# A grouped convolution with two attention gates: the convolution put on eight array tiles, the column sums folded, the statistics made one unit earlier

## The reference

```python
def _gn(v, G=32, eps=1e-5):                # over 16 channels and all pixels
    return (v - mean) / sqrt(var + eps)

# per group gx [16, 128, 128] of the normed x
ch = conv1x1(concat(mean(gx), max(gx)), w_cc, b_cc)       # 32 -> 16, one value a channel
channel_weight = sigmoid(norm_over_1x1(ch, gn1_w, gn1_b))
hw = conv1x1(concat(mean over columns, mean over rows), w_s1, b_s1)
pos_h = sigmoid(conv1x1(hw[rows], w_ph, b_ph))            # one value a channel and row
pos_w = sigmoid(conv1x1(hw[columns], w_pw, b_pw))         # one value a channel and column
sx = conv3x3(gx * pos_h * pos_w, w_s3, pad 1) + b_s3      # 16 -> 16 channels
spatial_weight = sigmoid(norm_per_channel(sx, gn2_w, gn2_b))
out = x + gx * channel_weight * spatial_weight
```

## Time and profile before

| | |
|---|---|
| median of 3 runs | 4297.24 us (4292.31 to 4298.69) |
| the profiled execution, its time | 4296.2 us |
| its span, first to last instruction | 4294.3 us |
| mean granted TensorE clock | 0.965 of full speed |
| HBM read, written | 268.64 MB, 268.44 MB |

### The profile page before, as it was taken

One profiled execution on the slowest core, in us unless ns is written; L12 is line 12 of the kernel. 1 busy time (PEld: TensorE's weight loads), 2 busy tenths in 40 slices (PEclk: granted clock), 3 DMA queues, 4 the chain that ended last, 5 costly groups with the idle time before them and its releaser, 6 DMA issues.

```text
span 4294.3 us, 55492 instructions
## 1 busy us (share of the span) xinstructions
PE 4041.4 (94%) x11016; PEld 1938.2 (45%) x11016; DVE 4018.4 (94%) x2719; ACT 2624.4 (61%) x4354; POOL 1775.4 (41%) x2314
## 2 busy tenths in 40 slices
PE   5999999999999999999999999999999999999997
PEld 2444444444444444444444444444444444444443
DVE  7999999999999999999999999999999999999996
ACT  3566566666665666666656666666666666665665
POOL 3443444444434434443344434344444344434443
PEclk9999999999999999999999999999999999999998
DMA  6777777777777777777777777777777777777775
GB/s 124 163 173 173 172 175 169 175 172 173 172 173 169 177 173 172 175 167 178 172 172 172 172 176 172 171 172 176 168 177 173 172 175 167 177 173 173 171 177 123
DMA packets 1147751, 730.57 MB, mean 170 GB/s; under 512 B 74144, under 2 KB 1122976, under 8 KB 1147552
## 3 DMA queue, kind: packets, MB, share of 16 engines
q1 hardware_dynamic: 1147552, 728.87, 74.7%
HBM read 268.64 MB, written 268.44 MB: 125 GB/s over the span
## 4 chain that ended last, share of the span: by engine, by line
DVE 53%; issue 18%; SPq 11%; DMA 9%; PE 6%; POOL 1%; ACT 1%; DVEq 1%; POOLq 0%; ACTq 0%
DVE sums L560 13%; DVE mx L607 12%; SPq L222 11%; DMA xt<-in_x 9%; DVE sp_buf L524 7%; DVE sums L554 7%; DVE gated L567 7%; DVE sp_buf L527 6%; PE conv_ps L637 5%; POOL rstd L275 1%; ACT sp_buf L416 1%; DVE gate_hr L594 0%; PE pos_ps L637 0%; DVE ch L603 0%; DVE sums_n L545 0%
## 5 line engine op out<-in xcount | busy, mean ns | idle before, releaser
L637 PE MATMUL conv_ps<-gated,W_conv 128*128 128x512 f32 x6144 | 2973.1, 619 | 16.5 <-DVE gated L567 16.3
L637 PEld LDWEIGHTS conv_ps<-gated,W_conv 128*128 128x128 f32 x6144 | 1143.4, 197 | 1100.0 <-issue 1071.7
L637 PE MATMUL conv_ps<-halo,W_halo 96*128 96x512 f32 x2048 | 1027.7, 604 | 2.1 <-DMA halo<-gated 1.6
L370 ACT ACTIVATE sp_buf<-conv_ps,weights 128x1024 f32<-128x1024 f32 x512 | 565.3, 1104 | 747.8 <-PE conv_ps L637 747.5
L323 POOL TENSOR_TENSOR gated<-gate_w,gate_hr 128x2048 f32<-128x2048 f32 x256 | 918.7, 3609 | 166.9 <-DVE gate_hr L594 157.6
L560 DVE TENSOR_REDUCE sums<-xt 128x128 f32<-128x2048 f32 x256 | 943.6, 3725 | 0.0
L554 DVE TENSOR_REDUCE sums<-xt 128x16 f32<-128x2048 f32 x256 | 584.2, 2282 | 171.5 <-DMA xt<-in_x 171.4
L524 DVE SCALAR_TENSOR_TENSOR sp_buf<-xt,negm,sp_buf 128x2048 f32<-128x2048 f32 x256 | 600.6, 2346 | 38.3 <-ACT sp_buf L416 38.3
L527 DVE SCALAR_TENSOR_TENSOR sp_buf<-sp_buf,kfac,xt 128x2048 f32<-128x2048 f32 x256 | 602.1, 2352 | 9.0
L567 DVE SCALAR_TENSOR_TENSOR gated<-xt,negm,gated 128x2048 f32<-128x2048 f32 x256 | 593.9, 2361 | 0.0
L343 POOL TENSOR_TENSOR rstd<-var_e,consts 128x2 f32<-128x2 f32 x128 | 89.8, 701 | 1176.8 <-DVE var_e L581 1176.8
(11 more groups left out here) (79 smaller groups left out, 2174.4 us busy)
## 6 DMA issues: line engine op xcount, KB each, us to landing
xt<-in_x SPq DMA_DIRECT2D x2048, 128.0 KB, 3.0
out<-sp_buf SPq DMA_DIRECT2D x2048, 128.0 KB, 2.5
halo<-gated SPq DMA_DIRECT2D x512, 365.2 KB, 6.0
weights<-in_by_channel SPq DMA_DIRECT2D x1, 116.5 KB, 2.6
S_chan<-in_same_channel SPq DMA_DIRECT2D x1, 64.0 KB, 1.9
whalo_in<-in_wconv SPq DMA_DIRECT2D x2, 3.0 KB, 1.8
masks<-in_row_masks SPq DMA_DIRECT2D x1, 12.0 KB, 1.9
hmask<-in_halo_mask SPq DMA_DIRECT2D x1, 3.0 KB, 1.9
```

What stands on the lines that cost most here:

```text
L370: nc.scalar.activation(sp_buf[:, g, k * 8:k * 8 + 8], conv_ps[:, h % 2], ACT.Identity, bias=V["b_s3"], accum_out=ssum2[:, g, k:k + 1]).the ...
L637: return nc.tensor.matmul(ps, lhsT, rhs, start=start, stop=stop)
```

## The change

- **Partitions.** Partition p now is channel (p % 32) // 2 and row 2 (p // 32) + p % 2. Rows 0 to 3 of all channels are partitions 0 to 63, and the outputs of a pair of rows are one strip of 32 partitions.
- **Convolution.** gated has a band of zeros above and below (NB + 2). Each 128 x 128 matmul is replaced by eight with 64 rows and 32 columns of the weights (`tiles`), the one for row 7 into row 0 reading a band higher, the one for row 0 into row 7 a band lower. So halo, its DMAs and its matmuls are gone. conv_ps is four banks; slot n does the lower four tiles for bank n and the upper four for bank n - 1, kw by kw, and the evacuation is by bank: eight a unit of 512 columns.
- **Column sums.** Two additions of halves (16 bands to 8 to 4), and the last 4 are added by four accumulating matmuls. The mean is subtracted by matmuls as well (W_rows_m, W_cols_m), so sums_n is gone.
- **Channel norm.** GpSimd's channel_in and channel_norm are gone. The input is three matmuls on raw values; ScalarE does the norm (`channel_variance`, `channel_gate`), and the power is taken in one GpSimd instruction with the next unit's rstd.
- **Order.** Row sums, maxima and folds are of e = t + 3, mean, squares, variance and positions of c = t + 2. Both groups of b are finished at the end of VectorE's body. Slots XS = 6, load(j) fetches unit t + 5, and the loop has six bodies.

```diff
-                halo_rows(0)
-                halo_rows(1)
@@ GpSimd, body
+                    rstd2_power(b, sb_, 0)
+                    gate_products(a, sa, 0)
+                    gate_products(a, sa, 1)
+                    end_factor(t, q)
+                    rstd2_power(b, sb_, 1)
+                    rstd_power(c, sc)
@@ ScalarE, channel norm and body
+            def channel_variance(u, s):
+                act.wait_ge(ch_mm, u + 1)
+                for j in range(2):
+                    nc.scalar.activation(ch[:, 0, j:j + 1], cw_ps[:, j:j + 1], ACT.Identity,
+                                         scale=rstd[:, s, j:j + 1], bias=V["b_cc"]).then_inc(ch_var, 1)
+                for j in range(2):
+                    act.wait_ge(ch_var, 6 * u + j + 1)
+                    nc.scalar.activation(ch[:, 1, j:j + 1], ch[:, 0, j:j + 1], ACT.Identity, scale=-1.0,
+                                         bias=ch[:, 0, j:j + 1]).then_inc(ch_var, 1)
+                act.wait_ge(ch_var, 6 * u + 4)
+                nc.scalar.activation(ch[:, 2], ch[:, 1], ACT.Square).then_inc(ch_var, 1)
+                act.wait_ge(ch_var, 6 * u + 5)
...
+                nc.scalar.activation(var_e[:, (s + 1) % 2, 2:4], ch[:, 2], ACT.Identity,
+                                     bias=consts[:, 4:5]).then_inc(ch_var, 1)
+            body: variance2(b, 0); gates(a); mean1(c); square1(c, 0); evacuate(b, 7); square1(c, 1);
+                  evacuate(t, 0); spatial_gate(b, 0); evacuate(t, 1); square2(b, 1); evacuate(t, 2);
+                  evacuate(t, 3); channel_variance(a); variance2(b, 1); evacuate(t, 4);
+                  spatial_gate(b, 1); channel_gate(a); evacuate(t, 5); square2(t, 0); evacuate(t, 6)
@@ VectorE
+            def fold_columns(u, s, j):
...
+                nc.vector.tensor_tensor(fold8[:], xt[:, s, j, 0:8], xt[:, s, j, 8:16],
+                                        ALU.add).then_inc(fold8_done, 1)
+                dve.wait_ge(fold8_done, n + 1)
...
+                nc.vector.tensor_tensor(fold4[:, s % 2, j], fold8[:, 0:4], fold8[:, 4:8],
+                                        ALU.add).then_inc(fold4_done, 1)
+            body: row_sums(e, 0); scaled_row_gate(a); row_sums(e, 1); totals(e); channel_maxima(c);
+                  maxima(e); modulate(a, 0); modulate(a, 1); variance1(c); fold_columns(e, 0 and 1);
+                  gate_x(b, 0); add_x(b, 0); gate_x(b, 1); add_x(b, 1)
@@ TensorE
+                        mm(pos[:, :, 0:NB], W_rows[:, :], sums[:, dc], stop=False)
+                        mm(pos[:, :, 0:NB], W_rows_m[:, :], shift.to_broadcast([P, 2, NB]), start=False)
+                        for i in range(4):
+                            mm(pos[:, :, NB:NB + W], W_cols[:, :], fold4[:, dc, :, i], start=i == 0, stop=False)
+                        mm(pos[:, :, NB:NB + W], W_cols_m[:, :], shift.to_broadcast([P, 2, W]),
+                           start=False).then_inc(pos_mm, 1)
+                def tiles(u, d, n, half, kw, start):
+                    j, k = n // BANKS, n % BANKS
+                    for o in range(PAIRS):
+                        band = 1 + BB * k
+                        if half == 1 and o == 0:
+                            band -= 1
+                        if half == 0 and o == PAIRS - 1:
+                            band += 1
+                        rows = slice(ROW_TILE * half, ROW_TILE * (half + 1))
+                        cols = slice(QUAD * o, QUAD * (o + 1))
+                        ins = mm(conv_ps[cols, k], W_conv[rows, kw, cols],
+                                 gated[rows, d, j, band:band + BB, kw:kw + W], start=start and kw == 0,
+                                 stop=not start and kw == KW - 1)
+                    return ins
+                def slot(n, first=0, last=KW):
...
+                        if n % BANKS == 0:
+                            pe.wait_ge(mod_done, 2 * t + n // BANKS + 1)
+                        if later(8 * t + n, BANKS):
+                            pe.wait_ge(evac, 8 * t + n - BANKS + 1)
...
+                    for kw in range(first, last):
+                        if real(t):
+                            ins = tiles(t, q % 2, n, 0, kw, True)
...
+                            if n > 0:
+                                ins = tiles(t, q % 2, n - 1, 1, kw, False)
+                            else:
+                                ins = tiles(b, sb_ % 2, 7, 1, kw, False)
+            body: mean(c); maxima(c); var2(b, 0); slots 0, 1, 2; mean2(b, 1); channel(a); slot 3;
+                  variance(c); positions(c); slots 4, 5; var2(b, 1); slot 6; mean2(t, 0); slot 7
```

More of the change, by code:

```diff
@@ L525, in finish, with add_x @@
+            def add_x(u, s, j):
+                g = 2 * (s % 2) + j
+                n = 2 * u + j
+                flat = sp_buf[:, g].rearrange("p b w -> p (b w)")
                 dve.wait_ge(fin_a, n + 1)
                 dve.wait_ge(kfac_done, u + 1)
-                nc.vector.scalar_tensor_tensor(flat, flat, kfac[:, s, j:j + 1], xf, ALU.mult, ALU.add).then_inc(final, 1)
-            def body(t, q):
+                nc.vector.scalar_tensor_tensor(flat, flat, kfac[:, s, j:j + 1],
+                                               xt[:, s, j].rearrange("p b w -> p (b w)"),
+                                               ALU.mult, ALU.add).then_inc(final, 1)
@@ new lines, in row_sums, with totals @@
+            def row_sums(u, s, j, come):
+                dve.wait_ge(x_in[s][j], come)
+                if later(u, 2):
+                    dve.wait_ge(pos_mm, u - 1)
+                nc.vector.tensor_reduce(sums[:, s % 2, j], xt[:, s, j], AX_X, ALU.add).then_inc(sums_done, 1)
+            def totals(u, s):
+                dve.wait_ge(sums_done, 2 * u + 2)
+                if later(u, XS):
+                    dve.wait_ge(ch_mm, u - XS + 1)
+                nc.vector.tensor_reduce(tot[:, s], sums[:, s % 2], AX_X, ALU.add).then_inc(tot_done, 1)
@@ new lines, in scaled_row_gate, with modulate @@
+            def scaled_row_gate(u, s):
+                dve.wait_ge(gates_done, 4 * u + 4)
+                dve.wait_ge(rstd_done, u + 1)
+                if later(u, 2):
+                    dve.wait_ge(gp_done, 2 * (u - 1))
+                nc.vector.tensor_tensor(gate_hr[:, s % 2], gate_h[:, s % 2],
+                                        rstd[:, s, 0:2].unsqueeze(2).to_broadcast([P, 2, NB]),
+                                        ALU.mult).then_inc(ghr_done, 1)
+            def modulate(u, s, j):
+                dve.wait_ge(gp_done, 2 * u + j + 1)
+                inner = gated[:, s % 2, j, 1:1 + NB, 1:1 + W]
+                nc.vector.scalar_tensor_tensor(inner, xt[:, s, j], negm[:, s, j:j + 1], inner,
+                                               ALU.add, ALU.mult).then_inc(mod_done, 1)
@@ L615, in body @@
-                modulate(0)
-                modulate(1)
-                if real(b):
-                    finish(b, sb_, 1)
+                e, se = t + 3, (q + 3) % XS
+                if real(e):
+                    row_sums(e, se, 0, loads(k, q, 3))
+                if real(a):
+                    scaled_row_gate(a, sa)
+                if real(e):
+                    row_sums(e, se, 1, loads(k, q, 3))
+                    totals(e, se)
+                if real(c):
+                    channel_maxima(c, sc)
@@ new lines, in body @@
+                if real(e):
+                    maxima(e, se)
+                if real(a):
+                    modulate(a, sa, 0)
+                    modulate(a, sa, 1)
+                if real(c):
+                    variance1(c, sc)
+                if real(e):
+                    fold_columns(e, se, 0)
+                    fold_columns(e, se, 1)
+                if real(b):
+                    for j in range(2):
+                        gate_x(b, sb_, j)
+                        add_x(b, sb_, j)
```

585 lines of the change are left out of this document (257 added, 328 removed).

## The result

| | before | after |
|---|---|---|
| median | 4297.03 us (4292.31 to 4298.69) | 4090.01 us (4088.28 to 4098.33) |
| span of the profiled execution | 4294.3 us | 4088.5 us |
| mean granted TensorE clock | 0.965 | 0.939 |

The account below looks back on a forecast made before the run. TensorE at 29.0 us a unit, just above the store loop's 28.7, was to bound, with a period of 29.1: 33 + 63.5 + 124 x 29.1 + 92 = 3797, plus 3, gives 3800 us; range 3615 to 4170.

Parts of the forecast that it names:

- The tiles: TensorE's convolution: eight tiles stream together, 2.57 us a slot plus 5% for feeding, 2.70 a slot, 21.6 us a unit.
- The mode switches: TensorE, five places a unit with small matmuls between slots: array shape changes twice at each, 0.25 us taken, 2.5 in all.
- tiles feed slowly: Rival on TensorE's convolution: slots of 2.9 to 3.2 us, TensorE alone bounds, 3980 to 4265 us, still faster; chance 0.14.
- do not feed: Rival on TensorE's convolution: each small pass costs a fixed 117 ns, 52.4 us a unit, 6.7 ms, slower; chance 0.10.
- go in order: Rival on TensorE's convolution: passes stay in order, 0.428 us a tile matmul, 89.7 us a unit, 11.3 ms; chance 0.04.
- The wait for x: VectorE's wait for loaded x, 1.3 us a unit before the change, was to go wholly.
- The wait for the sigmoid: VectorE's gate_x waits for the spatial gate's sigmoid, about 1 us, if the store loop closes.
- ScalarE's work: ScalarE's busy time a unit: 20.5 us, plus 1.1 for evacuations and 3.2 for the channel norm, 24.8.
- store loop: SP's loads and stores, then evacuate(t, 4), spatial gate, gate_x, next finish: 57.4 us for two bodies, 28.7 each.
- the loops listed ahead of it: Two cross-engine loops: store loop, 28.7 us; and channel_maxima through channel(), slots, sigmoid, gate_x and add_x, 27 to 29 us.
- The rival with ScalarE's queue as bound: ScalarE: small activations take 0.39 us and evacuations wait for stores, 30 to 31.5 us a unit, 3910 to 4095; chance 0.08.
- VectorE against GpSimd: Modulates on VectorE blocked by GpSimd's gate products: 0.2 us a unit if the gates are in time, 3.3 if not.

Follow-up runs that it names:

- a3: Kernel after with the squares of (t, 0) moved ahead of channel_gate on ScalarE and SP issuing each store ahead of its load: 3825.9 us, ratio 0.8901.
- a7: Kernel after with VectorE's folds between its two group finishes and the squares of (t, 0) ahead of channel_gate: 3804.5 us, ratio 0.8853.
- a1: Kernel after with ScalarE's squares of (t, 0) moved ahead of channel_gate and evacuate(t, 5): 4007.84 us, ratio 0.934.
- a8: Kernel after with folds between the group finishes, squares ahead of channel_gate, and stores issued ahead of loads: 3793.12 us, ratio 0.8826.
- a4: Kernel after with the folds replaced by one strided reduction a group and one matmul in place of four: 4189.79 us, ratio 0.9748.
- b1: Kernel before with its strided column sums replaced by four additions a group at the same place in VectorE's order: 4896.99 us, ratio 1.1401.
- a2: Kernel after with useless matmuls of about 0.9 us put ahead of the mean on TensorE: 4074.18 us, ratio 0.948.
- a10: Kernel after with useless matmuls ahead of the mean and VectorE's gate_x and add_x each split in two halves: 4063.64 us, ratio 0.9466.
- a11: a8 with twelve bodies to a turn of the hardware loop on every engine but SP: 3757.86 us, ratio 0.8748.

## Why the prediction was wrong in size

- **The tiles: right.** A slot was taken at 2.70 us, and is 2.74. The mode switches were too dear: a small matmul beside tiles takes 0.31 us, one among others 0.24. TensorE's unit at full clock is 27.7 for the 29.0 of the sum. The rivals in which tiles feed slowly, do not feed, or go in order, are out.
- **VectorE: right.** 3529.2/128 = 27.6, for 27.5. The wait for x is gone. The wait for the sigmoid was named, at about 1 us; it is 3.3 in the steady unit.
- **ScalarE's work: near.** 3011.4/128 = 23.5 for 24.8.
- **The step that failed is the period, "Bounds on the period: VectorE 27.5, store loop 28.7, TensorE 29.0. Taken: 29.1".** Steadily it is 30.9. Of the loops listed ahead of it, none holds the squares of (t, 0): the order puts them behind the sigmoid of (b, 1), channel_gate and an evacuation, and the third small matmul of TensorE's next body waits for them. The words "plus waits in order: close to the others, not above" put this at nothing without following it. The ring makes TensorE stand 1.5 us (0.8 in a3 and 0.5 in a7, where the squares stand ahead), and the clock then takes 1.7 more. The clock was named as something that might fall ("Granted clock as before; if it falls, TensorE's terms double where it does") and had no term.
- **The rest.** The forecast's span was 3797, the profiled one is 4088.5. The steady period is 123 x (30.89 - 29.1) = 220 of the difference, the loop's turns 123 x (31.26 - 30.89) = 46, the first body and the tail the remaining 26: to tot of body 0, 82.14, the start went as predicted (33 + 13 + 13.5 + 18.5 + 4.8 = 82.8), but body 0 took 28.2 and not 18.5, and from the last tot to the end are 133 us and not 116.
- **The store loop** was put at 28.7, with four blocks of DMA issues at 23.8 us. Here they take 26.3, from 2005.07 to 2031.37, which by the same sum makes it 30.0:

```profile
2005.07 6.67 SPq L225 DMA_DIRECT2D xt<-in_x  x8
...
2025.32 6.05 SPq L233 DMA_DIRECT2D out<-sp_buf  x8
```

  In the kernel after it costs 60.0 us of wait at most; with the ring cut it was the next thing in the way (a1 against a3).
- **The rival with ScalarE's queue as bound** gave 3910 to 4095 us, and the result lies in it. Its mechanism was another: its evacuations waiting for stores. What it had right is that an engine busy 74% can set the period by its order.
- **VectorE against GpSimd** was costed for the modulates alone, at 0.2 us a unit. The pair that matters is a power of one column behind a gate_x, an add_x or a fold, 0.5 to 1.7 us wherever it falls so, and it sits in the ring.

The forecast's 3800 us is within reach of this change: a8, with only orders changed, runs at 3793.12. That both figures lie so close is partly luck: 29.1 is 0.9 above a8's steady period of 28.19, while the turns of the loop, which had no term, body 0 and the tail came out longer.

## What to carry to other kernels

Work out engine sums, but then follow each matmul at the head of a body back through the other engines' orders until it meets TensorE again; a ring of small steps can set the period although no engine in it is full. Put what a ring waits for ahead of what nobody waits for (here one line, 82 us; with the two other orders 297). Cost each two-input VectorE instruction by what GpSimd does at that moment, and the other way round: two additions a group gain 100 us behind the products (a4 against the kernel after), and four lose 600 beside them (b1).

## What the runs showed that was not expected

- A wait of TensorE of 1.5 us was mostly followed by a stretch at 1.2 GHz that costs 1.7 us; one of 0.5 or 0.6 us (a2, a8) never was. The wait alone does not decide it: in the kernel after the clock fell in 92 of 100 units, behind waits of 1.33 to 3.20 us, and stayed up in 8, behind 1.25 to 2.65; in a10 it stayed up behind waits of up to 2.88. What else decides is not shown.
- Making VectorE's instructions half as long made the kernel slower by 69 us: GpSimd's power met them in another phase and was held by 0.8 us in the commonest unit.
- A turn of the hardware loop costs 5 us with six bodies (a8) and 6.1 to 6.5 with twelve (a11): TensorE stands some 3 us, and the clock is at half behind it.
- The two passes of one fp32 matmul on a tile do not hold the other tiles: 48 passes of 512 columns in 2.74 us are 57 ns each, with eight tiles at work, where a full-array pass takes 428 ns.
